# Attention operands of a head group: sixteen 16-partition gathers become six, with one 8 KB run per partition

## The reference

```
Q = poincare_fully_connected(x, z_q, b_q)     # x @ z, then arcsinh / sinh per feature, then one factor per position
K = poincare_fully_connected(x, z_k, b_k)
V = x @ w_v.T + b_v
scores = einsum('bhqd,bhkd->bhqk', Qh, Kh) / 4      # 16 heads of 16 dimensions
out = einsum('bhqk,bhkd->bhqd', softmax(scores), Vh)
```

## Time and profile before

| | |
|---|---|
| median of three runs | 3173.93 us |
| the profiled execution, its own time | 3171.44 us |
| its span, first to last instruction | 3169.6 us |
| PE (matmul) busy | 2838.4 us, 90% |
| ACT busy | 2026.5 us, 64% |
| DVE busy | 1846.0 us, 58% |
| POOL busy | 1273.0 us, 40% |
| DMA queue of SP | 163840 packets, 198.25 MB, 28.4% of 16 engines' span |
| gathers, b_st<-b_scratch | 512 transfers of 128 KB, median 7.0 us from issue to landing |
| stores, b_scratch<-b_parts | 32 transfers of 768 KB, median 7.7 us |

### The profile page before, as it was taken

How to read it: one execution, slowest core, us unless ns; L and a number is a source line. 1 busy time by engine, 2 the same in 40 slices (tenths; PEclk the granted TensorE clock), 3 DMA queues, 4 the chain that set the end, 5 groups by cost and what they waited for, 6 DMA issues and landing times. The chain is left out here.

```text
span 3169.6 us, 38539 instructions
## 1 busy us (share of the span) xinstructions
PE 2838.4 (90%) x12161; PEld 1226.5 (39%) x12161; DVE 1846.0 (58%) x2420; ACT 2026.5 (64%) x2650; POOL 1273.0 (40%) x786
## 2 busy tenths in 40 slices
PE   3899999999979999657999999999999999969997
PEld 1455555555554444322323232323233332234443
DVE  8899999999973453454443444444444441144444
ACT  6454555455425555325889797978878889835554
POOL 4798899889861220141314131322313230021210
PEclk7899999999999999778999999999999999989999
DMA  2010001010012211206263635535553627231112
GB/s 80 1 37 27 30 26 36 23 33 26 24 56 75 80 53 53 67 11 132 29 146 42 134 54 94 93 73 92 92 94 58 116 46 128 27 114 48 60 53 67
DMA packets 163998, 200.30 MB, mean 63 GB/s; under 512 B 16504, under 2 KB 118272, under 8 KB 163840
## 3 DMA queue, kind: packets, MB, share of 16 engines
q1 hardware_dynamic: 163840, 198.25, 28.4%
HBM read 139.49 MB, written 58.72 MB: 63 GB/s over the span
## 5 line engine op out<-in xcount | busy, mean ns | idle before, releaser
L1859 ACT ACTIVATE b_pr<-b_ps 128x1024 f32<-128x1024 f32 x1024 | 1002.8, 1025 | 255.5 <-PE b_ps L1956 251.2
L1956 PE MATMUL b_ps<-b_st 128*128 128x512 bf16 x2048 | 591.2, 386 | 71.0 <-DMA b_st<-b_scratch 31.6
L1938 PE MATMUL b_acc<-b_pr,b_vaug 128*32 128x512 f32 x4096 | 549.0, 608 | 0.4 <-ACT b_pr L1859 0.4
L1956 PEld LDWEIGHTS b_ps<-b_st 128*128 128x128 bf16 x2048 | 150.3, 98 | 649.5 <-ACT b_pr L1859 381.9
L1257 PE MATMUL f_po<-f_s,f_w 128*128 128x512 f32 x768 | 355.0, 605 | 9.4 <-DVE f_xr L1042 5.9
L1030 DVE TENSOR_TENSOR f_turned<-f_cs,f_s 128x1024 f32<-128x1024 f32 x96 | 119.3, 1243 | 364.4 <-ACT f_cs L1159 359.4
L635 PE MATMUL a_pv<-a_xnT,a_wv 128*128 128x512 f32 x512 | 251.2, 614 | 52.8 <-DVE a_mem L403 38.7
L1123 ACT ACTIVATE f_h<-f_po,f_b 128x512 f32<-128x512 f32 x192 | 131.9, 687 | 218.1 <-PE f_po L1257 218.1
L627 PE MATMUL a_pu<-a_xnT,a_wk 128*128 128x512 f32 x512 | 238.3, 609 | 29.2 <-DVE a_frac L355 23.2
L1575 POOL TENSOR_TENSOR b_SQ<-b_A 128x1024 f32<-128x1024 f32 x32 | 64.7, 2021 | 467.1 <-DVE b_A L1672 467.1
L674 PE MATMUL a_py<-a_wo,a_out 128*128 128x256 f32 x960 | 229.1, 382 | 0.0
(11 more groups left out here) (259 smaller groups left out, 4694.4 us busy)
## 6 DMA issues: line engine op xcount, KB each, us to landing
b_st<-b_scratch SPq DMA_DIRECT2D x512, 128.0 KB, 7.0
b_scratch<-b_parts SPq DMA_DIRECT2D x32, 768.0 KB, 7.7
f_xl<-x SPq DMA_DIRECT2D x16, 1024.0 KB, 5.5
f_xr<-x SPq DMA_DIRECT2D x16, 1024.0 KB, 6.8
a_xl<-in_L_attn_a_x_dram SPq DMA_DIRECT2D x16, 512.0 KB, 4.2
x<-a_xr SPq DMA_DIRECT2D x32, 256.0 KB, 2.2
x<-f_xr SPq DMA_DIRECT2D x8, 1024.0 KB, 4.5
b_xl<-x SPq DMA_DIRECT2D x8, 1024.0 KB, 7.8
```

The costliest lines, as they stand in the source:

```text
L1859: nc.scalar.activation(pr[:, 4 * (blk % 2) + j, :], ps[:, j % 2, :], ACT.Exp, scale=SC).then_inc(S["probs_done"], 1)
L1938: x = nc.tensor.matmul(acc[32 * j:32 * j + 32, h * 512:(h + 1) * 512], vaug[:, kt, c:c + 32], pr[:, 4 * (kt % 2) + j, h * 512:(h + 1) * 51 ...
L1956: x = nc.tensor.matmul(ps[:, j % 2, h * 512:(h + 1) * 512], st[:, g % 2, 1, j, kt * P:(kt + 1) * P], st[:, g % 2, 0, j, h * 512:(h + 1) * ...
```

## The change

The features of Q and K are put into another order, and the gather is written with six transfers.

The DRAM tensor gets the order [Q or K, part, group, dimension, head in group, position]. For one part, group and dimension the four heads' rows follow each other, so they make one run of 8 KB. A gather now has three transfers for Q and three for K. They fill 48, 48 and 32 partitions, each partition with one run of 8 KB. For Q a transfer reads the same part three (or two) times, for K it reads the parts 0 to 2 (or 0 to 1). In all of them the outer dimension on the DRAM side is the 16 dimensions of a head, and the copies or parts are the second one. Inside such a stack the order of partitions is therefore dimension first and pair second, for Q and K alike. The bytes moved stay 2 MB per group.

So that `parts` can be stored with the same row-by-row transfer as before, the features must lie on the partitions in the order (group, dimension, head). A new tile `zp` is a copy of `z_sb` with its columns in this order, made by one ScalarE activation of 128 x 1024 elements ahead of the first Tanh. The squares and the projections read `zp`, and VectorE waits for it. The bias columns are loaded in the same order by eight transfers of 64 values instead of four of 128.

```diff
-Q_PART = [0, 0, 0, 1, 1, 1, 2, 2]
-K_PART = [0, 1, 2, 0, 1, 2, 0, 1]
+Q_RUNS = [(0, 3, 0), (3, 3, 1), (6, 2, 2)]
+K_RUNS = [(0, 3, 0), (3, 3, 0), (6, 2, 0)]
...
-    scratch = nc.dram_tensor("b_scratch", [2, 3, D, T], BF16, kind="Internal").ap()
+    scratch = nc.dram_tensor("b_scratch", [2, 3, H // 4, DK, 4, T], BF16, kind="Internal").ap()
...
+        zp = s.sb("zp", [P, 2, KD, D])
...
-        N_W = 16 * 8
-        N_G = 16 * 16
+        N_W = 16 * 12
+        N_G = 16 * (len(Q_RUNS) + len(K_RUNS))
...
             for o in range(2):
-                sp.dma_start(scratch[o, :, f * P:(f + 1) * P].rearrange("w p t -> p w t"), parts[:, o, :, f, :])\
+                sp.dma_start(scratch[o, :, 2 * f:2 * f + 2].rearrange("w g d j t -> (g d j) w t"), parts[:, o, :, f, :])\
                     .then_inc(parts_stored[f], 16)
...
-            for o, part in enumerate((Q_PART, K_PART)):
-                for i, w in enumerate(part):
-                    sp.dma_start(st[i * DK:(i + 1) * DK, slot, o],
-                                 scratch[o, w, 64 * g:64 * g + 64, :].rearrange("(h d) t -> d h t", d=DK))\
-                        .then_inc(st_loaded[slot], 16)
+            for i, n, w in Q_RUNS:
+                sp.dma_start(st[i * DK:(i + n) * DK, slot, 0].rearrange("p h t -> p (h t)"),
+                             scratch[0, w, g].rearrange("d h t -> d (h t)").unsqueeze(1).broadcast_to([DK, n, 4 * T]))\
+                    .then_inc(st_loaded[slot], 16)
+            for i, n, w in K_RUNS:
+                sp.dma_start(st[i * DK:(i + n) * DK, slot, 1].rearrange("p h t -> p (h t)"),
+                             scratch[1, w:w + n, g].rearrange("w d h t -> d w (h t)")).then_inc(st_loaded[slot], 16)
...
                 for o, r in enumerate((bq, bk)):
-                    for f in range(KD):
-                        sp.dma_start(rcol[:, 2 * o + f:2 * o + f + 1],
-                                     r[f * P:(f + 1) * P].rearrange("(p o) -> p o", o=1)).then_inc(S["w_loaded"], 16)
+                    for g in range(G):
+                        c = 2 * o + g // 2
+                        sp.dma_start(rcol[g % 2 * 64:g % 2 * 64 + 64, c:c + 1],
+                                     r[64 * g:64 * g + 64].rearrange("(j d) -> d j", d=DK),
+                                     allow_slow_non_contiguous=True).then_inc(S["w_loaded"], 16)
...
                 dve.wait_ge(S["w_loaded"], N_W)
-                nc.vector.tensor_tensor(A[:, 0, :], z_sb[:].rearrange("p o k n -> p (o k n)"),
-                                        z_sb[:].rearrange("p o k n -> p (o k n)"), ALU.mult).then_inc(S["setup_v"], 1)
+                dve.wait_ge(S["z_done"], 1)
+                nc.vector.tensor_tensor(A[:, 0, :], zp[:].rearrange("p o k n -> p (o k n)"),
+                                        zp[:].rearrange("p o k n -> p (o k n)"), ALU.mult).then_inc(S["setup_v"], 1)
...
                 act.wait_ge(S["w_loaded"], N_W)
+                nc.scalar.activation(zp[:].rearrange("p o k (g d j) -> p (o k g) d j", g=G, d=DK),
+                                     z_sb[:].rearrange("p o k (g j d) -> p (o k g) d j", g=G, d=DK), ACT.Copy).then_inc(S["z_done"], 1)
...
-                            x = nc.tensor.matmul(bank, z_sb[:, q // 2, k, (q % 2) * P:(q % 2 + 1) * P], xnT[:, k, c],
+                            x = nc.tensor.matmul(bank, zp[:, q // 2, k, (q % 2) * P:(q % 2 + 1) * P], xnT[:, k, c],
                                                  start=k == 0, stop=k == KD - 1)
```

More of the change, by code:

```diff
@@ L1424, in phase_b @@
         zn2, zn2m = cols[:, 3, :], cols[:, 4, :]
-        names = ("w_loaded setup_p setup_v setup_a setup_m xl_loaded xr_loaded stored stats_done mv_done rstd_done "
+        names = ("w_loaded z_done setup_p setup_v setup_a setup_m xl_loaded xr_loaded stored stats_done mv_done rstd_done "
                  "xn_done lam_done dlam_done misc_ready misc_taken inT_done a_done sq_done root_done abs_done y_done ln_done e_done "
```

## The result

The changed kernel took 3163.24 us (median of five runs, 3158.63 to 3163.84) against 3174.24 us of the kernel before beside it: ratio 0.9956, 95% interval 0.9941 to 0.9971. The forecast was 3160, its own range 3151 to 3167. The profiled execution has a span of 3161.4 us and took 3163.24 us.

The account below looks back on a forecast made before the run. ScalarE's exponentials were taken to bound each batch. A quicker first gather (6.4 us) less setup (0.7) plus shorter jump-backs (8) gave 13.7 us less: 3157.7 as profiled, 3160 us as median, range 3151 to 3167.

Parts of the forecast that it names:

- What bounds: ScalarE's exponentials bound each batch, 131 us; a quicker gather pays only before the first scores and at the loop's jump-backs.
- The gather, -6.4: Before the first scores: issue to scores takes 10.25 us instead of 16.65, saving 6.4 us.
- The interpolation by the number of partitions: First gather's rate, estimated between 16 partitions (140 GB/s) and 128 (360): 256 GB/s for 48 partitions, 213 for 32.
- the old 1.65 us: Start and landing of the first gather, beside 15.0 us of transfer before; kept unchanged in the forecast.
- What is late next: First transpose after the first scores: no new wait for normalised `xl`; the first gather's saving capped at 6.9 us.
- The setup, +0.7: Start of phase b: bias transfers (2.5 us) and a 1.03 us copy cost 3.5 us, 2.8 covered by GpSimd, 0.7 left.
- The jump-backs, -8: Loop's four jump-backs: transfers end before PE stops, so stalls shorten and less clock is lost; 8 us saved.
- stand behind them: At the jump-backs, the code of the loop's first block seems to queue behind gather and store; PE restarts 2.5 and 2.1 us after.
- The sum: Whole kernel: 6.4 - 0.7 + 8 = 13.7 us less, forecast 3160 us (-0.43%).
- B: Rival: jump-back stalls don't care about the transfers' end, only 6.4 - 0.7 remain; 3168 us, chance 0.12.
- C: Rival: DRAM reading keeps the gather at 140 GB/s and the setup costs 0.7 us; 3174.6 us, chance 0.11.
- D: Rival: the six transfers use only 3 engines, so a gather takes 32.7 us; 3282 us, chance 0.08.

Follow-up runs that it names:

- e3_spread: Kernel before, each of the gather's 16 transfers filling every eighth partition instead of 16 neighbours; 3159.60 us, ratio 0.9960 to the kernel before.
- e9_spread32: Changed kernel, a gather being eight transfers of 32 partitions (every fourth) with 8 KB runs; 3158.04 us, ratio 0.9956 to the kernel before.
- e8_plain_copy: Changed kernel, z copied to zp in its own order instead of the new one, so the output is wrong; 3163.83 us (one run).
- e4_late: Changed kernel, store of half 1 issued three times, twice into a spare tensor; 3177.31 us, ratio 1.0013 to the kernel before.
- e5_unroll: Changed kernel, phase b's loop over batches 1 to 5 written out in straight code; 3144.39 us, ratio 0.9918 to the kernel before.
- e7_alt_unroll: Kernel before, gather on every eighth partition in order 0, 4, 1, 5, ..., loop over batches 1 to 5 written out; 3142.21 us, ratio 0.9902.
- e10_spread32_unroll: Changed kernel, gather in eight transfers on every fourth partition, loop over batches 1 to 5 written out; 3141.07 us, ratio 0.9907 to the kernel before.

## Why the prediction was right, step by step

*What bounds.* Right: only the first gather, the setup and the jump-backs moved. Away from these places the distance between an exponential and its counterpart in the other profile stays constant to a few hundredths of a microsecond.

*The gather, -6.4.* Right in sign and in cause, wrong in size: -3.8 and, in the second pair (the two repeated profiles), -3.5 us. The interpolation by the number of partitions (256 GB/s) was the step that failed; 208 were measured. That is 1.5 of the 2.6 us that are missing in the first pair. Most of the rest is a slower start, for which the sum had taken the old 1.65 us: in the first 2 us after the first issue 82 GB/s were moved, and 118 before. The interpolation asked how many partitions are written, and e3_spread shows that it matters which: 16 partitions with a step of 8 carry 207 GB/s at a share of 0.69, which would be 300 at full share (an estimate), where 16 neighbours carry 140 at 1.08. The Trainium skill (SBUF — State Buffer, Door 1: The DMA port swizzle) has four neighbours share a port. Its sum, which I had put beside mine, took the ports as evenly used, and came out as wrong as mine: with 8 ports for the first and last width and 12 for the middle one, 8.4 us, where 2.1 MB at 208 GB/s are 10.1 us. In the first transfer, by the same map of the Trainium skill, partitions 0 to 15 and 32 to 47 use the same four ports, which get twice the bytes of the other four; counted so, as an estimate from its figures, the sum is 9.6 us. That would explain most of the difference, but no run here took that apart.

*What is late next.* Right: no wait for `xl` at the first transpose, and none even in e9_spread32.

*The setup, +0.7.* Wrong in size: +2.45 us, +3.3 in the second pair (107.8 against 104.5 us to the first store). The weights landed 1.8 us later, where 2.5 were forecast. Two steps failed. The copy was priced by an exponential that reads its elements in order; the measured one is 0.9 us longer, and e8_plain_copy shows that the step is why. And I asked only who waits for GpSimd's root. The tensor engine, in order, makes the sums of squares ahead of the transposes; its sums now end at 1341.53, and the transposes, which had waited for `xl`, wait for them and start 1.1 us later (18.4 against 17.3 us after the first load; 3.1 us later in the second pair). Of the 2.45 us, 2.1 are there at the first projection (28.6 against 26.5 us); how 1.1 become 2.1, and the rest up to the store, I did not follow.

*The jump-backs, -8.* -11.6 and -9.5 us in the two pairs (43.0 and 41.8 before, 31.4 and 32.3 after). The forecast that the earlier end of the transfers would shorten the stalls to 2.4 us held, 2.15 to 2.6 us. It held by less than forecast: the transfers were to be over at 1773, and their last packet ended at 1779.9, 2 us before PE stopped. The reason given was half right. The stall is a fetch of code that the transfers hold up, but "stand behind them" is refuted by e4_late: only its start is put off, which makes 4.65 us of 2.2 and nothing beyond. The reading that PE restarts 2.5 and 2.1 us after the transfers' end was chance: their last packets end 0.6 to 1.9 us before the restart in the eight stalls of the two profiles before, the q8 packets 1.57 to 1.71 us. The Trainium skill (Runtime: NRT & Kernel Launch, Instruction fetch mechanics), cited in the prediction, says that such a branch forces a fetch by DMA; the trace agrees, with a q8 packet at every jump-back. The loss of clock stayed at three of the four (5.95 to 5.97 us from restart to the first transpose at a granted clock of 0.71; 4.71 us at the one where it was 1.00).

*The sum.* -13.7 forecast; -11.1 and -9.7 us in phase b of the two pairs, -11.0 us by the medians. The gather and the setup together come to almost nothing (-1.4 us and -0.2 us): nearly the whole gain is at the jump-backs, a place that no line of the diff touches. That the sum came out near is in part luck: gather and setup fell short by 4.3 us (5.5 in the second pair), and the jump-backs, taken at 8, gave 3.6 us more (1.5).

*The rivals.* B, C and D are out: the stalls shrank with the transfers and doubled with them in e4_late, the rate rose, and the engines' share was 1.01.

## What to carry to other kernels

A transfer into a few partitions should spread them over the memory: a step in the destination, which cost one edit here, gave as much as a new layout with a permuted weight. Then look at who waits for a transfer anywhere, and count the jumps of a hardware loop among those who do: each cost 2.2 us of standstill with idle transfers, 4.65 us under full ones, and in most cases more than a microsecond of low clock. The view of the DMA queues names the fetch of code (`instruction`), so an "issue" wait of this kind can be tested at once: ask it for the stretch around the stall. Writing out five batches gained another 0.4 to 0.6%, by the ratios of e5_unroll, e7_alt_unroll and e10_spread32_unroll to the same gathers with the loop; everything done to the gather gained 0.4%. No run wrote out the loop with the old gather.

## What the runs showed of the hardware that I had not expected

- 8 KB runs into 16 neighbouring partitions moved at 129 GB/s, 2 KB rows at 140: longer runs were no help.
- An issue of SP took 0.46 us for 16 neighbouring partitions and 0.63 us for 16 with a step, as much as for 48 partitions (0.62). With spread partitions this became the limit.
- At a loop's jump-back PE restarts 1.57 to 1.71 us after a 16 KB `instruction` packet on DMA queue 8 ends, in 40 of 40 cases. Transfers under way put off the start of this packet, from 0.4 us before PE's stop to 2.0 us after, and don't slow it down; the stall goes from 2.2 to 4.65 us and stays there (4 of 4 cases of e4_late).
- An activation copy of 128 x 1024 float32 reading with a step of 16 elements took 1.93 us, in order 1.06 us.
- The same program starts phase b anywhere from 1320.9 to 1323.4 us (before) and 1323.4 to 1325.8 us (after), and its first batch takes 164.6 or 165.9 us depending on when the granted clock rises.
